# Decay attention loop: query-state products for eight heads at once, in row halves of the array

## The reference, cut to what matters

```python
q = (x @ Wq).reshape(b, n, H, Dh).transpose(0, 2, 1, 3)     # H = 16, Dh = 64
k = (x @ Wk).reshape(b, n, H, Dh).transpose(0, 2, 1, 3)
v = (x @ Wv).reshape(b, n, H, Dh).transpose(0, 2, 1, 3)
q = _elu_plus_one(q)
k = _elu_plus_one(k)
a = jax.nn.sigmoid(x @ Wa + ba + 2.0)
def step(carry, inp):
    S, z = carry
    qt, kt, vt, at = inp
    S = at[..., None, None] * S + kt[..., :, None] * vt[..., None, :]
    z = at[..., None] * z + kt
    num = jnp.einsum('bhk,bhkv->bhv', qt, S)
    den = jnp.einsum('bhk,bhk->bh', qt, z) + eps
    return ((S, z), num / den[..., None])
...
return out @ Wo
```

## Time and profile before

| | |
|---|---|
| median of 3 runs | 1123.81 us (1123.32 to 1127.6) |
| the profiled execution, its own time | 1137.76 us |
| its span | 1136.0 us |
| mean granted TensorE clock over the span | 0.944 |
| PE busy | 1003.3 us (88%) |
| DVE busy | 752.2 us (66%) |
| ACT busy | 749.9 us (66%) |
| POOL busy | 431.6 us (38%) |

### The profile page before, as it was taken

One profiled execution on the slowest core, in us unless ns is written; L12 is line 12 of the kernel. 1 busy time (PEld: TensorE's weight loads), 2 busy tenths in 40 slices (PEclk: granted clock), 3 DMA queues, 4 the chain that ended last, 5 costly groups with the idle time before them and its releaser, 6 DMA issues. The chain is left out here.

```text
span 1136.0 us, 27259 instructions
## 1 busy us (share of the span) xinstructions
PE 1003.3 (88%) x10416; PEld 682.4 (60%) x10416; DVE 752.2 (66%) x1515; ACT 749.9 (66%) x1513; POOL 431.6 (38%) x573
## 2 busy tenths in 40 slices
PE   5889999999999999846898989999999998588993
PEld 3333333333333334546888976788787787488893
DVE  6789999999999998881222254766766766522223
ACT  4648888888888887444555457677677775544553
POOL 3742212221122211315556304555555552355651
PEclk9879999999999999978999968999999999699997
DMA  2233111111111100611111132121111120111113
GB/s 71 85 94 120 41 30 34 44 41 30 30 34 45 41 2 2 222 38 40 39 38 41 51 128 104 42 76 74 41 76 66 48 75 2 52 40 39 43 37 125
DMA packets 40039, 64.74 MB, mean 57 GB/s; under 512 B 10025, under 2 KB 21033, under 8 KB 37993
## 3 DMA queue, kind: packets, MB, share of 16 engines
q1 hardware_dynamic: 31736, 50.14, 13.7%
q0 software_dynamic: 4992, 10.23, 3.3%
q10 hardware_dynamic: 3184, 2.63, 0.7%
HBM read 47.86 MB, written 14.68 MB: 55 GB/s over the span
## 5 line engine op out<-in xcount | busy, mean ns | idle before, releaser
L803 ACT ACTIVATE PB<-S 128x512 f32<-128x512 f32 x576 | 308.5, 598 | 71.8 <-PE S L609 67.2
L915 DVE TENSOR_REDUCE mx<-S 128x2 f32<-128x1024 f32 (+1 forms) x192 | 207.7, 1130 | 8.6 <-PE S L595 8.6
L871 POOL TENSOR_SCALAR_AFFINE_SELECT PB<-PB 128x512 f32<-128x512 f32 x128 | 79.2, 637 | 307.7 <-ACT PB L803 307.6
L1527 DVE TENSOR_TENSOR m_hs<-m_gs,m_UP 128x512 f32<-128x512 f32 x78 | 53.7, 689 | 194.7 <-ACT m_gs L1363 119.3
L644 PE MATMUL PV<-PB,VP 128*32 128x256 f32 (+2 forms) x2432 | 178.2, 380 | 0.0
L609 PE MATMUL S<-W 50*128 50x512 bf16 (+3 forms) x768 | 124.1, 329 | 5.0 <-ACT PB L803 4.2
L1204 POOL DMA_INDIRECT yd_rows<-m_ys,m_target x78 | 76.8, 984 | 97.0 <-DVE m_ys L1534 87.8
L1257 PE MATMUL m_GP<-m_xt,m_wgu 128*128 128x128 f32 x624 | 87.8, 285 | 26.6 <-ACT m_xt L1359 20.7
L1359 ACT ACTIVATE m_xt<-m_XT 128x128 f32<-128x128 f32 x78 | 21.7, 278 | 128.5 <-PE m_XT L1248 100.1
L595 PE MATMUL S<-W 48*128 48x512 bf16 (+3 forms) x640 | 94.8, 327 | 13.1 <-DVE mx L911 4.9
L1257 PEld LDWEIGHTS m_GP<-m_xt,m_wgu 128*128 128x128 f32 x624 | 78.5, 197 | 32.4 <-issue 32.4
(11 more groups left out here) (328 smaller groups left out, 1918.4 us busy)
## 6 DMA issues: line engine op xcount, KB each, us to landing
d_LQ<-l_rows SPq DMA_DIRECT2D x15, 1024.0 KB, 4.9
W<-qk_parts SPq DMA_DIRECT2D x210, 32.0 KB
qk_parts<-OT SPq DMA_DIRECT2D x24, 256.0 KB, 3.0
W<-qk_parts SPq DMA_DIRECT2D x30, 96.0 KB
W<-in_L_ffn_w_gate SPq DMA_DIRECT2D x1, 2048.0 KB, 9.5
W<-in_L_ffn_w_up SPq DMA_DIRECT2D x1, 2048.0 KB, 14.5
xn_rows<-m_XN SPq DMA_DIRECT2D x8, 256.0 KB, 2.3
m_GB<-yd_rows SPq DMA_DIRECT2D x8, 256.0 KB, 5.9
```

Source lines behind the costliest of these rows:

```text
L803: nc.scalar.activation(PB[:, j % NPB, :], S2[:, j % 3, :], ACT.Exp, scale=SC).then_inc(exp_done, 1)
L871: nc.gpsimd.affine_select(out=tri, in_=tri, compare_op=ALU.is_ge, fill=0.0, base=0, pattern=[[0, U], [1, P]], channel_multiplier=-1).then_ ...
L915: nc.vector.reduce_max(mx[:, g % 2, c, :, heads[0], qb], S1[:, b, :, 0:w], AX.X)\
```

## The change

`across_chunks` is called for eight heads at once instead of four, and not in the slots, but right behind `scores`: `across_chunks(t, b, 1)` in slot 1 and `across_chunks(t + 1, 1 - b, 0)` in slot 3. Each head has a product of its own with the 64 rows of its half of the array and 65 columns, even heads into bank `OX`, odd heads into bank `TR`. The scaling by `eL` leaves `combine` and becomes `scaled(t, c)`, two operations for eight heads, which write into a larger `ox`; `combine` keeps the addition. Since `TR` is now shared by three users, `outputs_turn` and the first `keys_turn` wait for the scaling (`ox_ready`), and the order of values, turns and copies on TensorE and ACT is another.

```diff
         LAST_OUT, LAST_YTS = PA[:, 0], KT[:, NT % 2]
+        OXB = (OX[:], TR[:].rearrange("p j n -> p (j n)"))
...
                         pe.wait_ge(yn_done, t + 1)
+                        pe.wait_ge(ox_ready, t * 2 + 4)
...
-                def across_chunks(t, b, i):
-
+                def across_chunks(t, b, c):
+                    pe.wait_ge(kt_copied, t * 2 + 2)
+                    pe.wait_ge(elu_done, t * 4 + (3 + c))
+                    if c or from_(t, 1):
+                        pe.wait_ge(ox_ready, t * 2 + c)
+                    if from_(t, 1):
+                        pe.wait_ge(supd_done, t * 2 + (c - 1))
+                    for k in range(4):
+                        hp = 4 * c + k
+                        for a in range(2):
+                            q = slice(64 * a, 64 * a + 64)
+                            last = nc.tensor.matmul(OXB[a][:, k * VW:(k + 1) * VW], QT[q, b, hp, :], S[q, hp, a, :],
+                                                    start=True, stop=True)
+                    last.then_inc(inter_done, 1)
+
+                def within_chunk(t, b, i):
+                    pe.wait_ge(w_done, t * 4 + (i + 1))
                     if i or from_(t, 1):
                         pe.wait_ge(comb_done, t * 4 + i)
-                    if from_(t, 1) and i % 2 == 0:
-                        pe.wait_ge(supd_done, t * 2 + (i // 2 - 1))
-                    for j in range(2):
-                        hp = 2 * i + j
-                        last = nc.tensor.matmul(OX[:, 2 * j * VW:2 * (j + 1) * VW], QT[:, b, hp, :],
-                                                S[:, hp].rearrange("p h v -> p (h v)"), start=True, stop=True)
-                    last.then_inc(inter_done, 1)
...
                 def slot(t, b, i, last=False):
-                    across_chunks(t, b, i)
                     within_chunk(t, b, i)
                     if i == 1:
                         if not last:
                             state(t, b, 0)
                         scores(t, b, 1)
+                        across_chunks(t, b, 1)
                     elif i == 3 and not last:
                         scores(t + 1, 1 - b, 0)
+                        across_chunks(t + 1, 1 - b, 0)
...
-                    for c in range(2):
-                        if not last:
-                            values(n, nb, c)
-                        if not first:
-                            outputs_turn(t - 1, c)
+                    if not last:
+                        values(n, nb, 0)
+                        values(n, nb, 1)
+                    if not first:
+                        outputs_turn(t - 1, 0)
                     slot(t, b, 2)
-                    for c in range(2):
-                        if not last:
+                    if not first:
+                        outputs_turn(t - 1, 1)
+                    if not last:
+                        for c in range(2):
+                            queries(n, nb, c)
                             keys_turn(n, nb, c)
-                            queries(n, nb, c)
                     slot(t, b, 3, last)
...
                     exp_decay(t, b, 3)
+                    if not first:
+                        yt_copy(t - 1, 1)
                     if not last:
-                        for c in range(2):
-                            kt_copy(n, nb, c)
-                            exp_(n, 2 + c, 4 + c)
+                        exp_(n, 2, 4)
+                        kt_copy(n, nb, 0)
+                        kt_copy(n, nb, 1)
+                        exp_(n, 3, 5)
                         exp_decay(n, nb, 0)
...
+                def scaled(t, c):
+                    dve.wait_ge(inter_done, t * 2 + (c + 1))
+                    if from_(t, 1):
+                        dve.wait_ge(comb_done, t * 4 if c else t * 4 - 2)
+                    for a in range(2):
+                        last = nc.vector.tensor_tensor(ox[:, c].rearrange("p (k a) v -> p a k v", a=2)[:, a],
+                                                       OXB[a][:, 0:4 * VW].rearrange("p (k v) -> p k v", v=VW),
+                                                       eL[:, t, 8 * c:8 * c + 8].rearrange("p (k a) -> p a k", a=2)[:, a]
+                                                       .unsqueeze(2).to_broadcast([P, 4, VW]), ALU.mult)
+                    last.then_inc(ox_ready, 1)
...
                     combine(t, b, 1)
                     weigh(t, 2)
+                    scaled(t, 1)
                     if not last:
                         update(t, 0)
...
                         reciprocals(t, b)
                         weigh(n, 0)
+                        scaled(n, 0)
                     if not first:
                         add_out(t - 1)
```

More of the change, by code:

```diff
@@ L1630, in decay_attention @@
         WB = sb("WB", [P, 2, 2, 2, P])
-        ox = sb("ox", [P, 4, VW])
+        ox = sb("ox", [P, 2, 8, VW])
         O = sb("O", [P, 2, H, VW])
@@ L1731, in keys_turn @@
                             pe.wait_ge(v_done, 2)
+                            pe.wait_ge(ox_ready, 2)
                     for j in range(4):
@@ L1785, in scores @@
                         last.then_inc(at_done, 1)
-                def across_chunks(t, b, i):
-                    if i or from_(t, 1):
-                        pe.wait_ge(comb_done, t * 4 + i)
-                    if from_(t, 1) and i % 2 == 0:
-                        pe.wait_ge(supd_done, t * 2 + (i // 2 - 1))
-                    for j in range(2):
-                        hp = 2 * i + j
-                        last = nc.tensor.matmul(OX[:, 2 * j * VW:2 * (j + 1) * VW], QT[:, b, hp, :],
-                                                S[:, hp].rearrange("p h v -> p (h v)"), start=True, stop=True)
+                def across_chunks(t, b, c):
[11 more added lines that the diff above has]
+                                                    start=True, stop=True)
                     last.then_inc(inter_done, 1)
@@ L1800, in within_chunk @@
                     pe.wait_ge(w_done, t * 4 + (i + 1))
+                    if i or from_(t, 1):
+                        pe.wait_ge(comb_done, t * 4 + i)
                     for j in range(4):
@@ L1900, in _ @@
                 pe.wait_ge(e_ready, 4)
+                pe.wait_ge(v_done, 2)
+                across_chunks(0, 0, 0)
                 step(0, 0)
@@ L1965, in step @@
                     exp_decay(t, b, 2)
-                    for c in range(2):
[L1967 to L1970, removed]
+                    if not last:
+                        v_copy(n, nb, 0)
+                        v_copy(n, nb, 1)
+                    if not first:
+                        yt_copy(t - 1, 0)
                     exp_decay(t, b, 3)
+                    if not first:
+                        yt_copy(t - 1, 1)
                     if not last:
-                        for c in range(2):
-                            kt_copy(n, nb, c)
-                            exp_(n, 2 + c, 4 + c)
+                        exp_(n, 2, 4)
+                        kt_copy(n, nb, 0)
+                        kt_copy(n, nb, 1)
+                        exp_(n, 3, 5)
                         exp_decay(n, nb, 0)
@@ L2112, in elu_queries @@
                     if from_(n, 2):
-                        dve.wait_ge(inter_done, (n - 1) * 4)
+                        dve.wait_ge(inter_done, (n - 1) * 2)
                     for c in range(2):
@@ L2130, in combine @@
                         dve.wait_ge(yn_done, t - 1)
[L2131 to L2134, removed]
+                    dve.wait_ge(ox_ready, t * 2 + (i // 2 + 1))
                     nc.vector.tensor_tensor(O[:, b, 4 * i:4 * i + 4].rearrange("p h v -> p (h v)"), OI[:, 0:4 * VW],
-                                            ox[:].rearrange("p h v -> p (h v)"), ALU.add).then_inc(comb_done, 1)
+                                            ox[:, i // 2, i % 2 * 4:i % 2 * 4 + 4].rearrange("p h v -> p (h v)"), ALU.add)\
+                      .then_inc(comb_done, 1)
+                def scaled(t, c):
[8 more added lines that the diff above has]
+                    last.then_inc(ox_ready, 1)
                 def reciprocals(t, b):
@@ L2161, in update @@
                     dve.wait_ge(sd_done, t * 2 + (c + 1))
-                    dve.wait_ge(inter_done, t * 4 + (2 * c + 2))
+                    dve.wait_ge(inter_done, t * 2 + (c + 1))
                     for h in range(2):
@@ L2254, in _ @@
                 dve.wait_ge(cut_ready, 4)
+                scaled(0, 0)
                 step(0, 0)
```

## The result

The changed kernel takes 1148.18 us (median of 4 runs, 1143.02 to 1150.68), the kernel before 1124.57 on the same chip (4 runs, 1123.32 to 1127.6). The ratio is 1.0186, 95% interval 1.0144 to 1.0228: 23.6 us slower. The forecast was 1152 in a range of 1137 to 1163.

The account below looks back on a forecast made before the run. TensorE's instruction stream was taken to bound the loop at 17.05 us a step; the new chain makes it 18.96, 14 x 1.91 = 26.7, together +28 us on 1123.81, giving 1152 us, range 1137 to 1163.

Parts of the forecast that it names:

- The bound: Loop over 16 chunks: TensorE's instruction stream sets the pace, busy 17.10 of 17.10 us, one step 17.05 us.
- The price of the products: TensorE, per step: 1.80 us of old products removed, 1.86 us of new ones added, so the exchange counts zero.
- The lower end of 0.57: Lower bound for one new product group on TensorE: 0.57 us in place of 0.90, saving 0.66 a step.
- The chain: Waits across DVE, ACT and TensorE from one key projection to the next: step 18.96 in place of 17.05 us.
- The sum: Whole loop: chunks 1 to 14 at 1.91 us each give 26.7 us; with the end chunks together +28.
- about +1: Chunk 0: no outputs to turn, but its keys' turns have the same round trip, about 1 us more.
- The clock: Rival: holes in TensorE's stream bring the 1.2 GHz level for some stretches of the loop; 1160 to 1169 us, chance 0.10.
- The half chain: Rival: add_out doesn't hold state(t, 1), or ACT closes its gap; step 18.0 to 18.3, 1138 to 1143 us, chance 0.18.
- its gap of 0.75: Round trip copy, turn, copy between ACT and TensorE: 0.75 us before the second keys' copy starts at K+12.62.

Follow-up runs that it names:

- The swap back: The changed kernel's order, waits and two banks with the old products of 128 rows and 130 columns; ratio 1.0195 to the kernel before, step 18.58 us.
- the last run: Half-array products in the mended order, plus next chunk's first decays in ACT's gap, queries ahead of keys' turns, kt_copy between Relu and Exp; ratio 1.0040 to the kernel before.
- (c): The changed kernel with one move, the decays of slot 3 directly behind those of slot 2 on ACT; step 18.57 us, single execution 1109.66 us.
- the run with quadrants and the order mended: The changed kernel with quadrant products, two scalings and slot 3's decays moved, otherwise the order of the kernel before; ratio 1.0014 to the kernel before.

## Why the prediction was right

- *The bound.* TensorE set the pace before; the changed kernel has its holes where they were written. The forecast that its busy time would be about 17 of 19 was loose: it is 17.77 of 18.58, since the busy time covers the short holes.
- *The price of the products.* Counted at zero, taken from the scores' pairs and the 8-column row; forecast 0.93 us a group, measured 0.94. The swap back left the step at 18.58. The lower end of 0.57 did not hold. In the same place of the stream the old products take 1.00, so zero was about right. The 17.30 of the last run, above the old 17.05, doesn't show that the new ones cost more: that step still has a hole of about 0.2 us ahead of the next chunk's scores (they start 0.81 behind the within products, 713.74 to 714.55, where 0.62 is enough in the changed kernel). What halved the distance was halving the weight columns. The promise of up to twice the speed for a contraction of 64 rows, in the Trainium skill (TensorEngine Tiling (Array Packing), Overview), was not met here: 0.94 us for 1.00. The rule of the Trainium skill (TensorE: Matmul & The Clock Gate, LDWEIGHTS) that the load of weights takes time by their columns is what the runs agree with: 0.11 us a round with 128 weight columns, 0.06 with 64.
- *The chain.* Right in each link and its order. The step was 1.91 longer in the forecast, 1.53 in the trace. The term that was mis-sized is the scaling: two operations of 0.43 were taken as 0.86 in a row, but the first starts 0.08 before `weigh` has ended and the second 0.33 behind the first (816.07 to 816.40), so the pair ends 0.67 behind it. This stands twice in the chain. Of what the first pair saves, 0.15 are left at the decays and 0.11 at `weigh(n, 0)`. From there to `state(t, 1)` the forecast had 1.31 us and the trace 0.99, and `state` itself takes 0.62 for 0.57.
- *The parts of the loss.* Two moves show that the place of `scaled(n, 0)` costs 0.46 and that of `scaled(t, 1)` 0.31 a step; the new order without any sharing costs 0.74. Together 1.51 of 1.53. With its two scalings moved, the version that shares `TR` has the step of the one that doesn't, 17.80 and 17.79: there the sharing costs nothing beyond the places of the scalings. That the parts add up was read from these runs; no run shares `TR` in the order of the kernel before and leaves the scalings where the change has them.
- *The sum.* 28 us were forecast, 23.6 measured. The trace has 22: 19.3 from the start of the first key projection to that of the last, and 2.7 behind it (the last addition to `X` starts 31.5 us behind the last key projection before, 34.2 now). It is made up in another way than the forecast's. Ten steps lose 1.53 and every fourth, three in all, only 1.28, since those were 0.39 longer already before; behind the last key projection the loop loses 1.05 up to the last transposes. Together these are 20.2 where the forecast had 26.7. The first full distance loses 0.8, as the "about +1" said, and the very first is 0.6 shorter (it lies between 14.06 and 15.34 in all traces of this case, whatever the order). The last 1.6 us are the clock's.
- *The clock.* It stays at 1.00 in the steps, whose holes are short. In the last step the granted clock is 0.90 over 957 to 974.6 us, with a part at the 1.2 GHz level, where the last step of before had 1.00. From the last transposes on, the same operations take 6.9 us for 5.3, above all the last output projection, here before and now:

```profile
963.77 2.02 PE L1769 MATMUL d_SU<-d_WOX,d_YTS 128*128 128x136 f32 x16
```

```profile
968.60 3.22 PE L1772 MATMUL d_SU<-d_WOX,d_YTS 128*128 128x136 f32 x16
```

  This is not a fixed price of the new holes. (c), with the same step, kept 1.00 in its last step, and the run with quadrants and the order mended, with a step of 17.14, had 0.80. As a rival of its own (8 to 17 us) the clock did not come.
- *No rival decided.* The half chain (18.0 to 18.3) would have needed `state(t, 1)` not to wait for `add_out`, or ACT to close its gap of 0.75. Moving `scaled(n, 0)` behind `add_out` takes 0.46 off, so it does wait, and the gap stands in the timeline (822.32).

## What to carry to other kernels

When one engine is busy without a hole, an edit that adds waits to its stream has to be followed once around, link by link, to the same instruction of the next step; the slack of the other engines' sums (here 5 us of 17) says nothing, since a chain of 1.9 us can stand in it unseen. When a PSUM bank gets a new user, look at what stands behind the operation that empties it, and put that operation into its engine's idle time: two scalings moved past a neighbour gave back half of this loss. And before cutting a product to half the array, look which side sets its price: with fp32 weights of 128 columns and 8, 65 or 130 moving ones it was the weights' columns (0.12, 0.11 and 0.11 us from one start to the next), and fewer moving columns or rows bought next to nothing. Products of 512 moving columns, at 0.43 us, are another case.

## What the runs showed of the hardware

Four quadrants of 64x64 run side by side: 32 instructions of 65 moving columns in 0.62 us, with the seam (the short gap where products of another shape follow). Once it runs there is a start every 0.015 us, four to a round of 0.06. A floor near 0.03 for each instruction, one of the cases written down beforehand, isn't there.

A small DVE operation was about 0.33 us longer whenever it ran beside GpSimd's mask. In the kernel before, `reciprocals` starts with an operation on 16 columns. In 12 of 15 steps it starts while the mask runs, takes 0.50 us and ends together with it:

```profile
813.98 0.64 POOL L2032 TENSOR_SCALAR_AFFINE_SELECT d_DM<-d_DM 128x512 f32<-128x512 f32 x1
814.14 0.50 DVE L2142 TENSOR_SCALAR d_rd<-d_O 128x16 f32<-128x16 f32 x1
```

In the other three it comes behind the mask and takes 0.17:

```profile
796.54 0.64 POOL L2032 TENSOR_SCALAR_AFFINE_SELECT d_DM<-d_DM 128x512 f32<-128x512 f32 x1
...
797.47 0.17 DVE L2142 TENSOR_SCALAR d_rd<-d_O 128x16 f32<-128x16 f32 x1
```

The kernel with the order alone has the same twelve (0.49 or 0.50) and three (0.17). In the changed kernel the operation comes ahead of the mask (825.16 and 825.45) and takes 0.17 to 0.20 in all 15 steps. No run moved it by itself, so that the mask is the cause is read from the times alone.
